# Attention over a long context: maxima taken in pairs of PSUM banks, totals and weightings in longer runs

## What is computed

```python
q = rms_norm(linear(x, q_w, q_b), norm_q_w)            # 16 heads of 32
k, v         = text keys and values                    # 1344 per sequence
k_img, v_img = image keys and values                   # 257 per sequence
out = attention(q, k, v) + attention(q, k_img, v_img)  # two softmaxes, added
x = x + tanh(g_xattn) * linear(out, o_w, o_b)
x = x + tanh(g_ffn) * (routed experts(layernorm(x)) + shared expert(layernorm(x)))
```

## Time and profile before

| | |
|---|---|
| Median of three runs | 1830.33 us (1828.37 to 1831.3) |
| The profiled execution, its own time | 1831.94 us |
| Its span | 1830.7 us |
| PE busy in the span | 1764.8 us (96%) |
| DVE, ACT, POOL busy | 1181.2 us (65%), 824.2 us (45%), 904.4 us (49%) |
| Granted TensorE clock, mean | 0.993 |

### The profile page before, as it was taken

The page is one execution under the profiler, slowest core; times in us unless marked ns, Lnnn a source line. Parts: engine busy times, 40 slices in busy tenths (PEclk is TensorE's granted clock), DMA queues, the critical chain, the costliest instruction groups (busy, mean ns, idle before and its releaser), DMA issues. The chain is left out here.

```text
span 1830.7 us, 25272 instructions
## 1 busy us (share of the span) xinstructions
PE 1764.8 (96%) x9078; PEld 1113.7 (61%) x9078; DVE 1181.2 (65%) x2276; ACT 824.2 (45%) x1516; POOL 904.4 (49%) x335
## 2 busy tenths in 40 slices
PE   5999999999999999999999999998899999999999
PEld 4888878874444444444444445433576787888777
DVE  5776686677787767787677786745554445443465
ACT  4443323345555545555455564564221165555221
POOL 3222312116776654776456674665143376776552
PEclk9999999999999999999999999999999999999999
DMA  9556749446444553444453443401231467888432
GB/s 311 153 169 193 233 157 246 162 150 157 117 121 107 135 136 77 111 126 108 124 136 90 105 122 93 119 13 70 62 127 58 161 208 262 276 267 252 145 121 93
DMA packets 185253, 268.77 MB, mean 147 GB/s; under 512 B 24972, under 2 KB 122012, under 8 KB 184612
## 3 DMA queue, kind: packets, MB, share of 16 engines
q1 hardware_dynamic: 180008, 250.36, 47.0%
q0 software_dynamic: 5120, 16.78, 2.7%
HBM read 194.10 MB, written 105.93 MB: 164 GB/s over the span
## 5 line engine op out<-in xcount | busy, mean ns | idle before, releaser
L631 DVE TENSOR_REDUCE mp<-ps 128x1 f32<-128x512 f32 (+2 forms) x1024 | 531.1, 569 | 182.8 <-PE ps L434 177.5
L1092 ACT ACTIVATE P<-ps 128x512 f32<-128x512 f32 (+1 forms) x832 | 447.8, 597 | 333.5 <-PE ps L959 323.0
L1260 POOL TENSOR_TENSOR sacc<-sacc,P 128x2048 f32<-128x2048 f32 x80 | 368.3, 4603 | 74.9 <-ACT P L1092 66.6
L434 PE MATMUL ps<-Kst,Qst 96*128 96x512 f32 (+2 forms) x1024 | 383.8, 384 | 6.5 <-DVE mp L631 5.8
L434 PEld LDWEIGHTS ps<-Kst,Qst 96*128 96x128 f32 x1024 | 191.8, 188 | 259.9 <-DVE mp L631 211.9
L959 PE MATMUL ps<-Qst,Kst 100*128 100x512 f32 (+1 forms) x832 | 322.3, 408 | 9.7 <-ACT P L1092 9.7
L914 PE MATMUL ps<-P,Vg 128*32 128x512 f32 (+2 forms) x1792 | 238.3, 606 | 0.0
L803 POOL TENSOR_TENSOR cl<-craw,ch 128x1024 fp32r<-128x1024 f32 (+2 forms) x26 | 62.0, 2384 | 285.3 <-ACT ch L539 285.3
L959 PEld LDWEIGHTS ps<-Qst,Kst 100*128 100x128 f32 (+1 forms) x832 | 150.9, 186 | 76.9 <-ACT P L1092 35.0
L49 PE MATMUL ps<-W,ch 128*128 128x512 f32 (+1 forms) x408 | 162.4, 398 | 0.0
L51 PE MATMUL ps<-W,cl 128*128 128x512 f32 (+1 forms) x408 | 160.1, 393 | 0.0
(11 more groups left out here) (230 smaller groups left out, 2999.2 us busy)
## 6 DMA issues: line engine op xcount, KB each, us to landing
gur<-in_w_gate_up SPq DMA_DIRECT2D x23, 1024.0 KB, 7.8
Kst<-KHd SPq DMA_DIRECT2D x32, 640.0 KB, 8.0
Vd<-vf SPq DMA_DIRECT2D x50, 256.0 KB, 2.3
craw<-in_ctxT SPq DMA_DIRECT2D x24, 512.0 KB, 4.4
KHd<-sth SPq DMA_DIRECT2D x24, 512.0 KB, 3.5
KLd<-stl SPq DMA_DIRECT2D x24, 512.0 KB, 4.7
dnr<-in_w_down SPq DMA_DIRECT2D x23, 512.0 KB, 3.9
xg<-Xg SPq DMA_DIRECT2D x23, 512.0 KB, 8.0
```

Of the source, the lines that this page charges most:

```text
L434: pe.matmul(ps[:, bank, 0:c1 - c0], Qst[G % 3][0:96, j, 128 * qt:128 * qt + 128], Kst[G % 2][0:96, j, c0:c1], start=True, stop=True).then_ ...
L631: dve.reduce_max(mp[:, 4 * qt + j, c:c + 1], ps[:, bank, 0:c1 - c0], AX.X).then_inc(d_ra, 1)
L1092: act.activation(P[slot(G, kt)][:m, j, :], ps[:m, 2 + (e - 1) % 3, :], ACT.Exp, scale=SCALE).then_inc(a_exp, 1)
L1260: pool.tensor_tensor(sacc[:], x[:], P[slot(G, kt)][:], ALU.add).then_inc(g_sum, 1)
```

## The change

- **Maxima in pairs.** Text keys are cut in three equal parts of 448 instead of 512, 512 and 320. PE makes two products into two neighbouring banks, and one DVE reduction takes both maxima. There are 32 pairs a group, in two pairs of banks (0 and 1, 2 and 3). Scores have two banks (4 and 5) instead of three.
- **Weightings in runs.** Text tiles are weighted two at a time in every second step; the ends of text and image come in four further runs.
- **Totals.** Text tiles 0 to 8 are all summed off PE, tiles 0 to 7 by POOL (seven additions instead of six) and tile 8 by a new DVE addition, which raises `d_add`. PE makes 6 bursts of totals in a group instead of 8.
- POOL's first addition stands ahead of the two image multiplications instead of behind them. DVE's four reciprocals move from step 11 to steps 5 to 8, the text total from step 11 to step 12, and the copies of ACT between the second and third exponential of step 12. Tiles of the output projection go to steps 4, 6, 8 and 10.

```diff
-    CH = [(0, 512), (512, 1024), (1024, NTXT), (NTXT, NKP)]
+    CH = [(0, 448), (448, 896), (896, NTXT), (NTXT, NKP)]
...
-        dve.reduce_max(mp[:, 4 * qt + j, c:c + 1], ps[:, bank, 0:c1 - c0], AX.X).then_inc(d_ra, 1)
+        dve.tensor_reduce(pair_maxima(n), ps[:, bank:bank + 2, 0:c1 - c0], axis=AX.X, op=ALU.max).then_inc(d_ra, 1)
...
+    PAIRS = [3] * 10 + [2] + [0] * 2
+
+    def ra_bank(ra):
+        return 2 * (ra % 2)
...
+        def next_bank():
+            if ra >= 34:
+                pe.wait_ge(d_ra, ra - 1)
+            return ra_bank(ra)
...
-            if e > 3:
-                pe.wait_ge(a_exp, e - 3)
+            if e > 2:
+                pe.wait_ge(a_exp, e - 2)
...
+        def two_tiles(G, kt):
+            weigh(G, kt, 0, 128, kt == 0, False)
+            weigh(G, kt + 1, 0, 128, False, False)
+
+        def text_end(G):
+            pe.wait_ge(a_si, G) if G else pe.wait_ge(d_ones, 1)
+            total(G, 9, 0, 128, True, False)
+            weigh(G, 10, 0, 64, False, True)
+            total(G, 10, 0, 64, False, False)
+
+        def text_total(G):
+            pe.wait_ge(d_add, G + 1)
+            pe_heads(7, lambda j: ones[:, :], sacc, 0, 128, False, True).then_inc(p_tot, 1)
+
+        def image(G):
+            weigh(G, 10, 64, 128, True, False)
+            weigh(G, 11, 0, 128, False, False)
+            pe.wait_ge(a_txt, 2 * G + 2)
+            total(G, 10, 64, 128, True, False)
+            total(G, 11, 0, 128, False, False)
...
+            if kt in (3, 5, 7, 9, 11):
+                two_tiles(G, kt - 3)
...
-                if fk in (3, 5, 9, 10, 11, 12):
+                if fk < 8:
+                    act.wait_ge(g_sum, sum_no(fG, fk))
+                elif fk == 8:
+                    act.wait_ge(d_add, fG + 1)
+                else:
                     act.wait_ge(p_tot, tot_no(fG, fk))
-                else:
-                    act.wait_ge(g_sum, sum_no(fG, fk))
...
+            if kt == 11 and G < NG:
+                dve.wait_ge(a_exp, exp_no(G, 8, 3))
+                dve.wait_ge(g_sum, 7 * G + 7)
+                dve.tensor_tensor(sacc[:], sacc[:], P[slot(G, 8)][:], ALU.add).then_inc(d_add, 1)
...
-            if G < NG and kt - 1 in ON_POOL:
+            if G < NG and 2 <= kt <= 8:
                 add(G, kt - 1)
-            if kt == 1 and 1 <= G < NG:
+            if kt == 2 and 1 <= G < NG:
                 image_total(G - 1)
```

More of the change, by code:

```diff
@@ L466, in pe_project, with pair @@
         ra = 0
-        def units(i, part):
+        def pair(i, part):
             nonlocal ra
[L470 to L484, removed]
+            if pairs_behind(i - LAG - 1) + part >= pairs_behind(i - LAG):
+                return
+            if ra == 0:
+                pe.wait_ge(s_key[0][0], 48)
+                pe.wait_ge(s_qry[0], 48)
+                pe.wait_ge(a_tr, TR4)
+                pe.wait_ge(d_tr, TR4)
+            else:
+                pe.wait_ge(d_ra, ra)
+            if ra == PART1:
+                pe.wait_ge(s_key[0][1], 144)
+            pe_max_pair(0, ra, 0)
+            ra += 1
         pe.wait_ge(s_const, 48)
@@ L1021, in pe_attend, with scores @@
+            def place(i):
+                if i < len(pairs):
+                    pair(G + 1, pairs[i])
+            def scores(*js):
+                if G < NG:
+                    for j in js:
+                        score(G, kt, j)
             if kt == 0:
-                weighing()
                 place(0)
-                totalling()
+                if G:
+                    image(G - 1)
+                scores(0)
                 place(1)
+                scores(1)
                 place(2)
-                for j in range(4):
-                    if G < NG:
-                        score(G, kt, j)
-                    place(3 + j)
-            else:
-                if G < NG:
-                    score(G, kt, 0)
-                place(0)
-                if G < NG:
-                    score(G, kt, 1)
-                place(1)
-                if kt == 12 and more:
+                scores(2, 3)
+                continue
@@ L1039, in pe_attend @@
+            scores(0)
+            place(0)
+            scores(1)
+            place(1)
+            if kt == 1 and G:
+                image_end(G - 1)
+            if G == NG:
+                continue
+            if kt in (3, 5, 7, 9, 11):
+                two_tiles(G, kt - 3)
+            if kt == 12:
+                if G + 1 < NG:
                     pe.wait_ge(d_mn, 4 * (G + 2))
[L1040 removed]
+                    pe_mrow(next_bank())
                     ra += 1
[L1042 to L1043 removed]
```

272 lines of the change are left out of this document (104 added, 168 removed).

## The result

The changed kernel takes 1882.71 us (median of four runs, 1878.04 to 1884.05) against 1830.12 before, a ratio of 1.028 with an interval of 1.026 to 1.030: slower, as forecast, and 22 us more than the 1861 that was said, inside the range of 1841 to 1888.

What follows compares the result with a forecast made beforehand. PE bounds the kernel before; after, POOL's chain closes regular groups at 54.2 us instead of 52.2. Regular +22, long 0, first +1.5, last +8.4: together +32, 1864, median 1862, said 1861; range 1841 to 1888.

Steps and rivals of the forecast that it cites:

- What PE saves: Regular group: 2 of 22 bursts away and 18 runs down to 9; PE alone would save 4.7 us.
- PE's own work fits beneath: Regular group: PE's own work, 52.2 less 4.7, takes 47.5 us, under the 54.2 of POOL's loop.
- The head: From the text total to the end of tile 1's exponentials, before which POOL's first addition cannot start: 13.5 us.
- the chain: POOL's seven additions and two image multiplications in series after the head: 35.3 us, ending at 48.8.
- the tail: From POOL's seventh addition, through tile 11's exponentials, to the next text total at 54.2: 5.4 us.
- With only one pair ahead PE stalls: PE waits for DVE's pairs about 1.1 us each two steps, 4 to 5 a group, covered by POOL's 35.3.
- first rival: PE's saving comes through, group under 52.2 us; if POOL did not matter, 47.5 to 50 with stalls, 1781; chance 0.08.
- DVE's addition costs nothing: DVE's new addition, beside the tail, ends at 52.2, or 53.5 if the negation slips, under 54.2: no cost.
- Long groups: Three groups with output projection: PE adds four tiles in waiting steps, DVE takes 1.6 us more; 0, bounds -3 and +2 each.
- First group: POOL starts late with the projections' end; one addition more less the shorter PE work: +1.5 us.
- The clock: PE idles about 1.2 us in step 11; if over 3, the tail costs 3 to 4 us more, 1900; chance 0.03.
- second rival: DVE's addition and the stalls close the group: text total at 56 to 58, +42 to +66, 1885 to 1925; chance 0.12.

Runs made afterwards that it cites:

- e9: Changed kernel with POOL's additions covering 64 of 512 columns and DVE's attention maxima reading half of each bank's columns, both at once: 1831.76 us (0.999).
- e6: Changed kernel with only DVE's four reciprocals moved from steps 5 to 8 to step 12, computation whole: 1881.90 us (1.027).
- e2: Changed kernel with all seven POOL additions covering 64 of 512 columns (only the first group's first one whole): 1882.03 us (1.028).
- e3: Changed kernel with DVE's new addition (key tile 8) covering 64 of 512 columns: 1878.87 us (1.026).
- e5: Changed kernel with DVE's maxima reductions in the attention reading only the first half of each bank's columns: 1877.24 us (1.024).

## Why the prediction was right, point by point

- **What PE saves (4.7 us a group, "PE alone would save", and "PE's own work fits beneath" at 47.5).** Mis-sized. e9 shows 51.1 to 51.7 (51.2 in group 10), so PE's order saves 0.5 to 1.1. The removed bursts were counted at their full length and the rest of a step at the sum of its columns. But in e9 a step without a run takes 2.4 to 2.8 us, not 2.2 (four exponentials of 0.60 make 2.4), and one with a run 4.3 to 4.6, not 4.1. Steps 2 to 10 together take 30.8 instead of 5 x 2.2 + 4 x 4.1 = 27.4, which is 3.4 of the missing 3.7.
- **The head (13.5), the chain (35.3), the tail (5.4).** Right: 14.1, 35.1, 5.6. Where the chain closes alone (e6) it ends 47.65 us behind the copy; with after's 6.7 from there to the next copy that is 54.35, and the one interval of e6 at full clock is 54.38, forecast 54.2. The clock aside, the walk of POOL's loop is right to 0.2 us.
- **"With only one pair ahead PE stalls ... 4 to 5 in a group. POOL's chain covers that."** This is the step that failed. The stalls are there, as described, but steps 2 to 9 take 31.6 us with or without POOL, so POOL does not cover them. By the prediction's own numbers the loop of PE and DVE was 47.5 and 4 to 5, 51.5 to 52.5, safely under POOL's 54.2 (its first rival even says 47.5 to 50 "with stalls", which does not agree with that). Measured, it is 54.3 to 55.0. The stalls were not too small: from e9 to e2 they are 3.2 to 3.6 us, 1.2 of them for the four reciprocals between the pairs (e6). What was too small is the 47.5 beneath them. So the time came out nearly right by luck: the loop that was walked is 54.4, the loop that was left aside happens to be as long, and an experiment that only shortened the chain found nothing.
- **DVE's addition costs nothing, by less than a microsecond.** Right: 2.28 us (as long as in e2, beside an idle POOL), margin 0.5, and no gain in e3. The contention is in the rows: the copy of 16 columns took 2.07 us up to the end of POOL's addition, and 0.17 in e2, where POOL was idle. In most groups of e5 the addition itself waited:

```profile
1061.40 4.44 DVE L639 SCALAR_TENSOR_TENSOR mn<-mx,mn 128x16 fp32r<-128x16 f32 x1
...
1067.19 3.38 DVE L1193 TENSOR_TENSOR sacc<-sacc,P 128x2048 f32<-128x2048 f32 x1
```

  The Trainium skill (GPSIMD Engine Reference, section Specifications) states the sharing for VectorE's instructions with two SBUF inputs or in a two-port mode. The two rows of e5 have two inputs and agree with it; the copy has one, and the trace does not show in which mode it ran. In a regular group of after the contention cost nothing.
- **Long groups (0, bounds -3 and +2 each).** +1.5 each. In e5, with DVE's maxima halved, they take 61.4 to 61.5 instead of 65.6, less than before: it is DVE, with its maxima and its share in the four tiles, that ate PE's gain. The two were not separated.
- **First group (+1.5).** Missed, +8.0. POOL closes this group, before and after. The last line of its chain before, and the chain after:

```profile
431.15 14.00 POOL L1260 TENSOR_TENSOR sacc<-sacc,P 128x2048 f32<-128x2048 f32 x3
```

```profile
413.54 18.74 POOL L1243 TENSOR_TENSOR sacc<-sacc,P 128x2048 f32<-128x2048 f32 x4
432.23 2.38 POOL L1278 TENSOR_TENSOR Wol<-ot,Woh 128x1024 fp32r<-128x1024 f32 x1
434.56 2.38 POOL L1278 TENSOR_TENSOR Wol<-rt,Woh 128x1024 fp32r<-128x1024 f32 x1
436.89 9.22 POOL L1243 TENSOR_TENSOR sacc<-sacc,P 128x2048 f32<-128x2048 f32 x2
...
442.17 1.28 PE L961 MATMUL ps<-Qst,Kst 100*128 100x512 f32 x2 [3.14 <-ACT P L1086]
```

  The chain ends at 446.1 instead of 445.2: 1.0 us later, as good as forecast (the two subtractions for the output weights stand in it before as well). What the sum left out is the tail. Before, the text total stood right behind the last addition and its copy came 1.2 us later; after, it comes 8.2 us later, the 6.7 of a regular group and 1.5 more, for PE idled 3.14 us and then ran 6.8 us at the lower clock. The chain is the cause: in e2, where all additions here but the first are slivers, the copy comes 48.5 us behind the first score instead of 54.3 (46.3 before).
- **Last group (+8.4 with what follows).** Right: +6.9. Its six additions took 29.57 us instead of 28.12, beside the three subtractions; those were expected at 2.5 and cost 1.5.
- **The clock (0.03, "about 1.2 us only").** Right for regular groups of after. Where POOL alone closed the group (e5, e6) it fell in nearly every group, in e5 behind an idle time of 2.22 us, in e6 behind small ones only, and the run of four bursts took 3.0 to 3.2 us instead of 1.92.
- **The signs.** Four of six came as named. DVE's addition did not wait for POOL; the negation ahead of it did. And of "exponentials of tile 11 released by POOL, and PE idle before its third score of step 11" only the first half came; the missing half was the one that told POOL's loop from PE's. (One side sum is off: the second rival's +66 over the regular groups is 64 by its own 11 x 5.8; nothing hangs on it.)

## What to carry to other kernels

When two loops of different engines have nearly one length, a walk of one gives the right time and the wrong lever: removing either gains nothing, and only taking both away shows what they cost. So work out every loop of the group to its end, and look for idle time on the engine that the chain is said to hold: a wait on ACT without one on PE is no bound. Runs of the same kind of instruction save their switches, but leave the consumer of the other kind without input for the length of the run. Here, with one pair ahead, PE's new order alone was worth 0.5 to 1.1 us a group and the waits between PE and DVE cost 3.2 to 3.6.

## What the runs showed of the hardware

- In a row without gaps one DVE reduction over two banks of 448 takes 1.02 us, two single ones 1.08: the pair saves 0.06 us.
- A DVE copy of 16 columns took 2.07 us beside a GpSimd addition and 0.17 without one; in e5 an operation of the same size took 4.44 us. DVE's addition of 2048 columns took 2.28 us in after and in e2, and 3.37 to 3.38 in eleven groups of e5, where POOL's last multiplication ran beside it.
- PE's clock fell from its higher to its lower level (2.4 to 1.2 GHz, granted 0.5) behind 2.22 us of idle time in e5, where the earlier trace rows had shown 1.89 us without a fall. In e6 it fell at 1012.5 us, though no idle time of PE in the five us before was longer than 0.32 us; the same place of after (891.26, 893.69) has idle times of 0.32 and 0.21 us and kept the higher level, and so did one group of e6 itself (idle times of 0.31, 0.28 and 0.20 us). What tells the two apart was not found.
